# Query norms as one number per token and head, applied as the scale of the exponentials

## The reference

```python
q, k, v = split(x_shifted @ Wqkv)           # 16 heads of 64 each
q = q / max(norm(q), 1e-12) * q_scale
k = k / max(norm(k), 1e-12) * k_scale
q = q * cos * scale + rotate_half(q) * sin * scale
k = k * cos / scale + rotate_half(k) * sin / scale
sim = 8.0 * (q @ k2.T)                      # windows of 32 queries, 64 keys: own window and the one before
attn = softmax(where(mask, -big, sim))
out = (attn @ v2) @ Wo
```

## Time and profile before

| | |
|---|---|
| median of 3 runs | 5645.84 us (5634.64 to 5661.94) |
| profiled execution, its own time | 5646.26 us |
| its span, first to last instruction | 5644.5 us |
| mean granted TensorE clock | 0.916 |
| busy over the span | PE 84%, PEld 49%, DVE 65%, ACT 56%, POOL 36% |

### The profile page before, as it was taken

One profiled execution on the slowest core, in us unless ns is written; L12 is line 12 of the kernel. 1 busy time (PEld: TensorE's weight loads), 2 busy tenths in 40 slices (PEclk: granted clock), 3 DMA queues, 4 the chain that ended last, 5 costly groups with the idle time before them and its releaser, 6 DMA issues. The chain is left out here.

```text
span 5644.5 us, 160430 instructions
## 1 busy us (share of the span) xinstructions
PE 4758.0 (84%) x63808; PEld 2776.6 (49%) x63808; DVE 3687.3 (65%) x5172; ACT 3161.7 (56%) x9549; POOL 2036.1 (36%) x1438
## 2 busy tenths in 40 slices
PE   6888888677777689988988898889998899888886
PEld 3333333222223355655555565556555566555553
DVE  5666777433333577776777777777777677777764
ACT  4444444332322466666666666666666666666664
POOL 2212222100000444544544444444544444444441
PEclk9999999777777799999999999999999999999998
DMA  1000000000000433333334333343333333333332
GB/s 44 0 0 0 0 0 0 23 0 0 0 0 13 115 85 85 82 88 90 84 81 94 89 81 81 84 97 85 84 80 89 89 84 83 86 93 84 82 80 75
DMA packets 197282, 340.10 MB, mean 60 GB/s; under 512 B 63568, under 2 KB 63568, under 8 KB 195024
## 3 DMA queue, kind: packets, MB, share of 16 engines
q1 hardware_dynamic: 196560, 330.14, 24.9%
HBM read 34.19 MB, written 6.29 MB: 7 GB/s over the span
## 5 line engine op out<-in xcount | busy, mean ns | idle before, releaser
L377 ACT ACTIVATE c_Pb<-c_S,c_nb 128x64 f32<-128x64 f32 x3072 | 915.4, 326 | 848.1 <-DVE c_nb L659 848.1
L342 POOL TENSOR_TENSOR c_F<-c_tAB 128x1024 f32<-128x1024 f32 x384 | 907.0, 2362 | 362.3 <-DMA c_QK<-c_F 214.6
L330 POOL TENSOR_TENSOR c_Pb<-c_Pb,c_rs 128x512 f32<-128x512 f32 x384 | 400.3, 1042 | 1460.7 <-DVE c_rs L667 1460.7
L640 DVE SCALAR_TENSOR_TENSOR c_tAB<-c_PA,c_WP,c_base 128x1024 f32<-128x1024 f32 x384 | 492.4, 1282 | 366.3 <-PE c_PA L446 366.1
L377 ACT ACTIVATION_READ_ACCUMULATOR c_Pb<-c_S,c_nb 128x1 f32 x3072 | 673.1, 219 | 0.0
L655 DVE COPY c_VO<-c_PB 128x512 f32<-128x512 f32 x384 | 264.0, 688 | 477.3 <-PE c_PB L481 477.2
L481 PE MATMUL c_PB<-c_WV,xf 128*64 128x256 f32 x3072 | 452.2, 419 | 137.0 <-ACT c_sq L362 137.0
L334 POOL TENSOR_TENSOR c_sq<-c_sq 128x512 f32<-128x512 f32 x384 | 501.3, 1305 | 122.8 <-ACT c_sq L362 119.8
L640 DVE SCALAR_TENSOR_TENSOR c_tAB<-c_PB,c_WP,c_base 128x1024 f32<-128x1024 f32 x384 | 491.8, 1281 | 57.8 <-PE c_PB L446 54.7
L521 PE MATMUL c_S<-c_PTs,c_VE 64*64 64x32 f32 x10752 | 426.9, 221 | 59.4 <-DVE c_PTs L673 28.4
L647 DVE SCALAR_TENSOR_TENSOR c_F<-c_PD,c_F 128x1024 f32<-128x1024 f32 x384 | 466.8, 1216 | 8.9 <-ACT c_PD L368 8.8
(11 more groups left out here) (247 smaller groups left out, 9704.1 us busy)
## 6 DMA issues: line engine op xcount, KB each, us to landing
c_QK<-c_F SPq DMA_DIRECT2D x3072, 64.0 KB, 2.0
c_VE<-c_VO SPq DMA_DIRECT2D x384, 128.0 KB
c_VE<-c_VO SPq DMA_DIRECT2D x384, 96.0 KB
c_stage<-in_w_heads SPq DMA_DIRECT2D x24, 256.0 KB, 2.8
c_WT<-in_w_tails SPq DMA_DIRECT2D x6, 1024.0 KB, 6.6
a_W<-in_w_level SPq DMA_DIRECT2D x1, 3335.5 KB, 10.9
c_WT<-in_w_tails SPq DMA_DIRECT2D x6, 537.5 KB, 4.0
b_W<-in_w_level SPq DMA_DIRECT2D x1, 3133.0 KB, 10.2
```

The lines of the kernel that those rows point to most:

```text
L330: nc.gpsimd.tensor_tensor(p, p, rs[:, n % 2, :].unsqueeze(2).broadcast_to([P, HS, KEYS]), ALU.mult).then_inc(*p_ready.up())
L342: nc.gpsimd.tensor_tensor(F[:, j % 2], tAB[:, j % 2, 0], tAB[:, j % 2, 1], ALU.add).then_inc(*rotated.up())
L377: e = nc.scalar.activation(Pb[:, n % 2, i, :], S[:, n % 2, r, c * KEYS:(c + 1) * KEYS], ACT.Exp, bias=nb[:, n % 2, r * PS + c:r * PS + c + ...
L640: nc.vector.scalar_tensor_tensor(out=tAB[:, kind, half], in0=bank[:, :].unsqueeze(1).broadcast_to([P, 2, SEQ]), scalar=WP[:, 2 * kind + ha ...
```

## The change

Queries are no longer multiplied by the inverse of their norm. For an even job the squares become the weights of four matmuls, one per tile of 128 tokens, against a 128x4 matrix that picks the heads, so that the sums come out with tokens on partitions, 16 numbers for each. The logarithm, the exponential and the minimum work on these 16 columns, and the result is kept in rq. The rotated queries are permuted as they are. The scores are then those of the unscaled queries; `row_max` is followed by a 128x8 multiply of the maximum by rq, and each exponential takes rq as its scale and that product as its bias. Keys keep their path, with signals numbered by pairs of jobs. The diff, without the declarations of the new tiles, signals and the constant:

```diff
                 def permute(j, turn):
                     side, sub, kind = j // 4, j % 4 // 2, j % 2
-                    sp.wait_ge(*finished.nth(j + 1, turn))
+                    sp.wait_ge(*(finished if kind else rq_ready).nth(j // 2 + 1, turn))
...
                 def inverse_norm(j, turn):
                     act.wait_ge(*summed.nth(j + 1, turn))
+                    if j % 2 == 0:
+                        if j or not turn.first:
+                            act.wait_ge(*rq_ready.nth(j // 2, turn))
+                        nc.scalar.activation(lq[:, :], PD[:, 0:TILES * 4], ACT.Ln, bias=col["tiny"], scale=float(2 ** LN_SHIFT)).then_inc(*logs.up())
+                        act.wait_ge(*logs.nth(j + 1, turn))
+                        nc.scalar.activation(lq[:, :], lq[:, :], ACT.Exp, bias=col["shift"], scale=-0.5).then_inc(*rinvs.up())
+                        return
...
                 def exp(n, turn):
-                    act.wait_ge(*maxed.nth(n + 1, turn))
+                    side, t = divmod(n, TILES)
+                    act.wait_ge(*centred.nth(n + 1, turn))
...
-                                                 bias=nb[:, n % 2, r * PS + c:r * PS + c + 1], scale=1.0, accum_out=sums[:, n % 2, i:i + 1])
+                                                 bias=nr[:, n % 2, i:i + 1], scale=rq[:, side, t, i:i + 1], accum_out=sums[:, n % 2, i:i + 1])
...
                 def sumsq(j, turn):
                     pe.wait_ge(*added.nth(j + 1, turn))
-                    if j or not turn.first:
-                        pe.wait_ge(*finished.nth(j, turn))
-                    nc.tensor.matmul(PD[:, :], ones_head, sq[:, 0], start=True, stop=True).then_inc(*summed.up())
+                    if j % 2 == 0:
+                        if j or not turn.first:
+                            pe.wait_ge(*finished.nth(j // 2, turn))
+                        for t in range(TILES):
+                            mm = nc.tensor.matmul(PD[:, 4 * t:4 * t + 4], sq[:, 0, t * TILE:(t + 1) * TILE], const.heads, start=True, stop=True)
+                        mm.then_inc(*summed.up())
+                    else:
+                        pe.wait_ge(*rq_ready.nth(j // 2 + 1, turn))
+                        nc.tensor.matmul(PD[:, :], ones_head, sq[:, 0], start=True, stop=True).then_inc(*summed.up())
...
                 def finish(j, turn):
+                    dve.wait_ge(*rinvs.nth(j + 1, turn))
+                    if j % 2 == 0:
+                        sub = j % 4 // 2
+                        nc.vector.tensor_scalar(rq[:, j // 4, :, 4 * sub:4 * sub + 4], lq[:, :].rearrange("p (t h) -> p t h", t=TILES), 1.0 / NORM_MIN, None, ALU.min)\
+                            .then_inc(*rq_ready.up())
+                        return
                     dve.wait_ge(*rotated.nth(j + 1, turn))
...
                 def row_max(n, turn):
                     dve.wait_ge(*s_done.nth(n + 1, turn))
-                    nc.vector.tensor_reduce(nb[:, n % 2].rearrange("p (r c) -> p r c", r=2),
+                    side, t = divmod(n, TILES)
+                    nc.vector.tensor_reduce(nb[:, n % 2].rearrange("p (c r) -> p r c", r=2),
                                             S[:, n % 2, :, 0:PS * KEYS].rearrange("p r (c k) -> p r c k", c=PS),
                                             AX.X, ALU.max, negate=True).then_inc(*maxed.up())
+                    dve.wait_ge(*maxed.nth(n + 1, turn))
+                    if t == 0:
+                        dve.wait_ge(*rq_ready.nth(2 * side + 2, turn))
+                    nc.vector.tensor_tensor(nr[:, n % 2], nb[:, n % 2], rq[:, side, t], ALU.mult).then_inc(*centred.up())
```

More of the change, by code:

```diff
@@ L128, in network @@
         rs = sb("rs", [P, 2, HS])
+        nr = sb("nr", [P, 2, HS])
+        lq = sb("lq", [P, TILES * 4])
+        rq = sb("rq", [P, SIDES, TILES, HS])
         Pb = sb("Pb", [P, 2, HS, KEYS])
@@ L165, in network @@
         rotated = sig("rotated", JOBS)
-        finished = sig("finished", JOBS)
+        finished = sig("finished", JOBS // 2)
+        rq_ready = sig("rq_ready", JOBS // 2)
+        centred = sig("centred", NS)
         perm = [sig(f"perm{j}", 128) for j in range(JOBS)]
@@ L644, in finish @@
                 def finish(j, turn):
+                    dve.wait_ge(*rinvs.nth(j + 1, turn))
[4 more added lines that the diff above has]
+                        return
                     dve.wait_ge(*rotated.nth(j + 1, turn))
-                    dve.wait_ge(*rinvs.nth(j + 1, turn))
-                    nc.vector.scalar_tensor_tensor(out=F[:, j % 2], in0=PD[:, :].unsqueeze(1).broadcast_to([P, 2, SEQ]), scalar=1.0 / NORM_MIN,
-                                                   in1=F[:, j % 2], op0=ALU.min, op1=ALU.mult).then_inc(*finished.up())
+                    nc.vector.scalar_tensor_tensor(out=F[:, 1], in0=PD[:, :].unsqueeze(1).broadcast_to([P, 2, SEQ]), scalar=1.0 / NORM_MIN,
+                                                   in1=F[:, 1], op0=ALU.min, op1=ALU.mult).then_inc(*finished.up())
                 def v_copy(v, turn):
@@ L1642 @@
 C_ID, C_MEAN, C_HEAD, C_M64, C_TRI, C_CEN, C_MASK = (i * P for i in range(7))
-C_COL = C_MASK + 2 * PS * KEYS
+C_HOT = C_MASK + 2 * PS * KEYS
+C_COL = C_HOT + 4
 COLS = {"tiny": 2.0 ** -64, "shift": LN_SHIFT / 2 * float(np.log(2.0)), "eps5": 1e-5, "eps6": 1e-6}
@@ L1657, in __init__ @@
         self.cen = c32[:, C_CEN:C_CEN + P]
+        self.heads = c32[:, C_HOT:C_HOT + 4]
         self.mask = [c16[:, P + i * PS * KEYS:P + (i + 1) * PS * KEYS] for i in range(2)]
@@ L1865, in constants @@
     c[:, C_CEN:C_CEN + P] = np.eye(P) - 1.0 / P
+    c[:, C_HOT:C_HOT + 4] = np.arange(P)[:, None] // HALF == np.arange(4)[None, :]
     c[:, C_M64:C_M64 + P] = 1.0 / STATES
```

## The result

The changed kernel took 5777.06 us (median of 4 runs, 5766.89 to 5785.18), the kernel before, run beside it, 5641.05: a ratio of 1.0239, 95% interval 1.022 to 1.0259. Forecast was 5662 us, range 5620 to 5700. **Slower by 136 us, 2.8 us a turn, and outside the range.**

The account below looks back on a forecast made before the run. No one bound for the turn: TensorE, key transfers, VectorE or the gate chain by step. 0.19+0.12-0.47+0.37+0.12 = +0.33 us a turn, +16 us in 48 turns on 5645.84 us: 5662 us, range 5620 to 5700.

Parts of the forecast that it names:

- What is added on VectorE: Behind each row maximum, the 128x8 multiply makes VectorE's next operation 0.14 to 0.33 us late, 0.23 taken; counts only in step 4.
- Step 1, +0.19: Later exponentials delay the reciprocal and POOL's normalising, so the transposes start at 3524.71 instead of 3524.52: +0.19 us.
- Step 2, +0.12: Output copy behind the exponentials moves later, so job 7's keys' multiply starts at 3532.15, not 3532.03: +0.12 us.
- Step 3, -0.47: Query job 6's transfers issue about 1 us earlier, so job 7's key transfers start when its multiply ends: -0.47 us.
- Step 4, +0.37: VectorE-bound step; output copy and norm chain delays job 1's multiply to 3548.16 from 3547.79: +0.37 us in place of 0.23.
- Step 5, +0.12: On TensorE, a query job's sum as four small matmuls, halved figure plus one weight load, lies on the path: +0.12 us.
- Step 7, 0: Ends by TensorE's own order; the later exponentials and removed VectorE work were to change nothing.
- Step 6, 0: Starts after the gate chain and gelus; the reciprocal stands further behind the exponentials or the step waits otherwise: nothing.
- The second operand, 0.09 us taken: Exponentials' per-partition scale on ScalarE: 0 to 0.12 us each, 0.09 taken; 0.72 us a step, 0.96 with the late start.
- the exponentials become the bound: Rival: second operand costs 0.12 us, exponentials 1.20 us late; +1.05 us a turn, 5697 us; chance 0.22.

## Why the prediction was wrong

**The step that failed** is "What is added on VectorE". It priced the multiply from 0.14 to 0.33 us late, 0.19 long by the reciprocal (L667), "+0.23 there" in step 4, and nothing for what is queued behind it elsewhere. The length was right: 0.17 us where POOL is idle or the input lies in PSUM. But 383 of the 384 reciprocals start while POOL is idle, so that row could tell nothing of a wait for POOL. The multiply has two SBUF inputs, and in steps 2, 3, 5 and 7, and in 20 turns of step 4, it mostly started under POOL's add. There it took about 0.9 to 1.3 us, with the exponentials and all that hangs on them behind it; that is 1.5 of the 2.4%. The upper bound was taken from the nearest row by size, not by where its operands lie; the row that had them, L628 with 1.65 us, stood in the same turn. The section "Who interferes with whom" of the Trainium skill would have pointed to it.

**Point by point.**
- *Step 1, +0.19:* +0.29.
- *Step 2, +0.12:* +1.19; with the maxima in PSUM +0.10. The chain was the one described (output copy, norm, keys' multiply); only its start was wrong.
- *Step 3, -0.47:* -0.48. The transfers did start earlier. With the maxima in PSUM the scores' wait went from 43.9 us to 20.7, about half, as forecast; in the changed kernel, where step 2 is later by itself, to 5.5.
- *Step 4, +0.37:* +0.99; in PSUM +0.32. The median stands between two lengths: about +0.5 where the multiply is short, +1.4 where it waits for POOL's add.
- *Step 5, +0.12:* -0.21. The four small matmuls took 0.95 us where the two passes took 1.02, so nothing was added; and the row maximum of step 6 no longer waits for VectorE, whose queries' pass and copy had ended the step. The gelu behind it ends when it did, so step 6 gives this back.
- *Step 7, 0:* +0.50, gone in PSUM. Here the second gate product (`hidden(1)`) is queued behind the multiply, and TensorE's matmul L580 waits for it: 29.4 us in 48 waits, 11.9 in 7 with the maxima in PSUM. The forecast said such operations wait for TensorE anyway.
- *Step 6, 0:* +1.02, in PSUM +0.24, which is what step 5 gave. The rest is the clock: more turns at the lower mean (24 of 41 instead of 15; 15 in PSUM). Why is open.
- *The second operand, 0.09 us taken:* 0.084 (410 less 326). It is additive: 241, 327 and 411 ns with none, one and two. The Trainium skill, ScalarE: Activation LUTs, section "What ACT_TABLE_LOAD costs", gives about 93 ns each; the measurement is somewhat lower, and the Trainium skill was right that a second costs like the first.

With the multiply as priced, the sum of the medians holds: +0.34 us a turn against +0.33 forecast. In part that is luck: steps 1, 5 and 6 were missed by +0.12, -0.34 and +0.24, which cancel. And that kernel took 51 us more than before, not 16. By its trace the turns 1 to 6 of a layer are 0.33 us longer on average (from -0.6 to +1.7 by place in the layer, in one profile of each kernel), and the turns that load the next layer's weights 4.9 us (87.9 against 83.0). Step 7 of one of them, the maxima in PSUM and then the kernel before:

```profile
3750.92:3764.46 13.54, 11.85 (x158) 8.02 (x160) 7.66 (x13) 5.35 (x21) 4.62 (x3) 0.75 0.25 57
```

```profile
3730.92:3741.67 10.75, 8.82 (x152) 5.38 (x154) 8.36 (x12) 5.45 (x21) 4.63 (x3) 1.00 0.23 52
```

The granted clock is 0.75 on average instead of 1.00: part of the step ran at 1.2 GHz instead of 2.4, in four of the five such turns. Why it falls there was not tried, and is open; the prediction had no term for it. Of the rivals, "the exponentials become the bound" (5697 us) named a real piece, since the operand alone costs 0.77% in the kernel before, but it did so at 0.084 us, below the 0.1 it was said to need. None had the multiply wait for POOL.

## What to carry to other kernels

Before pricing a small VectorE instruction, ask where its inputs lie and what POOL is doing at that moment: two inputs in SBUF can make it as long as what is left of POOL's instruction (up to 1.58 us here, instead of 0.17), and a whole line of work waits with it. One input in PSUM took the wait away, and writing the maxima there cost next to nothing (695 ns instead of 687). And two delays on one chain are not to be priced apart: the first one may only use up the slack that hid the second.

## What the runs showed that I had not expected

- Where a POOL instruction was in flight at the multiply's start, the multiply ended 22 to 25 ns behind POOL's end (the middle half of 262 cases in the changed kernel); in the other 122 it took 169 ns at most.
- A fill on POOL, which reads no SBUF, did not hold it; an add or the rotation's sum did.
- Two SBUF inputs are not the only case. The layer norm's second operation (L722, one input, in SBUF like its output) took 0.49 us in the 22 turns of the changed kernel where POOL was idle at its start, and about 0.80 in the 26 where it was not, ending 0.28 us behind POOL; the two turns of step 4 above show one of each. Beside the fill it took 0.59. This was not tried further.
- A wait worth 0.36 points by itself (0.72 less 0.36) was worth 1.2 beside exponentials that are 0.7 us a step longer.
